# Three score banks in turned order, and the row of maxima in another of them, in an attention layer over 4,096 keys

## What is computed

```
energy = einsum('nqhd,nkhd->nhqk', q, k)            # 16 heads of 16 features
energy = where(mask == 0, -1e20, energy)            # one mask for both batches
attn   = softmax(energy / sqrt(256), axis=keys)     # over 4,096 keys
x      = x + (einsum('nhql,nlhd->nqhd', attn, v).reshape(...) @ w_out.T + b_out)
```

## Time and profile before

| | |
|---|---|
| median of 3 runs | 1079.19 us (1078.21 to 1080.05) |
| the profiled execution | 1083.97 us, its span 1082.3 us |
| PE busy | 964.2 us (89% of the span) |
| DVE busy | 595.2 us (55%) |
| ACT busy | 443.2 us (41%) |
| the units of layer 4 | from 458 us to 918 us of the span |
| time of one unit inside | 14.32 us (transposes of two units start at 701.51 and 715.83 us) |

### The profile page before, as it was taken

How to read it: one execution, slowest core, us unless ns; L and a number is a source line. 1 busy time by engine, 2 the same in 40 slices (tenths; PEclk the granted TensorE clock), 3 DMA queues, 4 the chain that set the end, 5 groups by cost and what they waited for, 6 DMA issues and landing times.

```text
span 1082.3 us, 19810 instructions
## 1 busy us (share of the span) xinstructions
PE 964.2 (89%) x7079; PEld 557.6 (52%) x7080; DVE 595.2 (55%) x1485; ACT 443.2 (41%) x812; POOL 97.5 (9%) x132
## 2 busy tenths in 40 slices
PE   6999989979899992599999999999999998755978
PEld 5888855545566662234444444444444443534547
DVE  3445434643122224677777777777777772294762
ACT  3443424521122210366666666666666665201011
POOL 1323210004011111000000000000000000100000
PEclk9999996989899997699999999999999999876998
DMA  7744865053003535825455444445555400800000
GB/s 273 241 160 172 321 264 223 2 187 98 11 30 115 157 128 113 180 37 74 74 74 72 68 65 65 62 65 72 72 72 72 68 6 20 187 0 1 0 1 20
DMA packets 76266, 106.09 MB, mean 98 GB/s; under 512 B 27478, under 2 KB 62647, under 8 KB 72186
## 3 DMA queue, kind: packets, MB, share of 16 engines
q1 hardware_dynamic: 70818, 89.38, 37.2%
q0 software_dynamic: 5200, 15.61, 3.7%
q10 hardware_dynamic: 200, 0.44, 0.1%
HBM read 83.40 MB, written 20.22 MB: 96 GB/s over the span
## 4 chain that ended last, share of the span: by engine, by line
PE 79%; DVE 5%; DMA 4%; issue 4%; ACT 4%; SPq 3%; ACTq 0%; POOL 0%; another core or an unknown queue 0%; POOLq 0%; DVEq 0%
PE bank L1191 12%; PE bank L1212 11%; PE bank L1200 8%; PE bank L1096 7%; PE bank L1169 5%; PE bank L1368 4%; PE bank L1120 4%; PE bank L903 3%; PE bank L890 3%; ACT region L805 2%; PE bank L985 2%; PE bank L1069 2%; PE bank L1223 2%; PE bank L994 1%; PE bank L1404 1%
## 5 line engine op out<-in xcount | busy, mean ns | idle before, releaser
L805 ACT ACTIVATE region<-bank 128x512 f32<-128x512 f32 x512 | 277.9, 595 | 173.4 <-PE bank L1200 173.4
L1690 DVE CUSTOM_DVE_ANT_0 xnT<-bank,region 128x1024 bf16<-128x1024 f32 x128 | 156.1, 1220 | 88.2 <-issue 88.2
L1191 PE MATMUL bank<-region 128*128 (+1 forms) x1024 | 163.4, 277 | 13.6 <-ACT region L805 12.6
L1690 DVE CUSTOM_DVE_ANT_0 region<-bank,region 128x1024 bf16<-128x1024 f32 x128 | 156.3, 1221 | 0.4
L1191 PEld LDWEIGHTS bank<-region 128*128 128x128 bf16 x1024 | 67.7, 97 | 139.8 <-ACT region L805 61.7
L1212 PE MATMUL bank<-region 128*32 128x256 f32 x2048 | 138.6, 385 | 0.0
L1200 PE MATMUL bank<-region,identb 64*64 64x512 bf16 x1024 | 105.4, 402 | 0.0
L1169 PE MATMUL bank<-region,xnT 64*128 64x512 bf16 x248 | 75.5, 385 | 5.0 <-DMA xnT<-region 5.0
L1212 PEld LDWEIGHTS bank<-region 128*32 128x32 f32 x2048 | 58.9, 109 | 34.2 <-ACT region L805 14.5
L1096 PE MATMUL bank<-region 128*128 x240 | 74.8, 465 | 1.2 <-DVE region L1612 1.2
L1171 PE MATMUL bank<-region,xnT 64*128 64x512 bf16 x248 | 75.5, 385 | 0.0
(11 more groups left out here) (317 smaller groups left out, 1151.1 us busy)
## 6 DMA issues: line engine op xcount, KB each, us to landing
region<-keys_split SPq DMA_DIRECT2D x224, 128.0 KB, 4.9
region<-in_ctx SPq DMA_DIRECT2D x32, 512.0 KB, 4.5
keys_split<-region POOLq DMA_DIRECT2D x48, 256.0 KB, 4.1
region<-in_L_ffn_we_gate SPq DMA_DIRECT2D x8, 688.0 KB, 8.7
region<-in_L_ffn_we_up SPq DMA_DIRECT2D x8, 688.0 KB, 9.8
region<-in_L_ffn_we_down SPq DMA_DIRECT2D x8, 640.0 KB, 9.3
region<-in_mask_1x1xSxS_ik SPq DMA_DIRECT2D x1, 4096.0 KB, 16.8
mask_kept<-region SPq DMA_DIRECT2D x1, 2048.0 KB
```

Of the source, the lines that this page charges most:

```text
L805: nc.scalar.activation(prob4[n % PROBS].rearrange("p a b -> p (a b)"), bank[:, SCORE4[n], :], ACT.Exp, scale=SCALE4).then_inc(exp4_ready, 1)
L1191: mm(bank[:, SCORE4[n], k * S:(k + 1) * S], slab[s][:, t * P:(t + 1) * P], qT4[:, bass.ds(u, 1), :].rearrange("p o q -> p (o q)"), start=( ...
L1690: v.tensor_tensor_reduce(out=junk[q], in0=bank[:, 3 + 2 * q:5 + 2 * q, :].rearrange("p a b -> p (a b)"), in1=maskN[:, q, 2 * c * CH:2 * (c ...
```

## The change

The order of the three banks is turned from half 8 on: the halves 8 to 15 take the banks 0, 2, 1, 0, 2, 1, 0, 2. The transposed maxima go into bank 1 (`NEG4`), and the wait ahead of them is for that bank's last half. `LAST_USE4` is worked out from the order by the same line as before, and so are all waits in `score_half`. No instruction is added or taken away.

```diff
-SCORE4 = (0, 1, 2, 0, 1, 2, 0, 1, 2, 0, 1, 2, 0, 1, 2, 1)
+SCORE4 = (0, 1, 2, 0, 1, 2, 0, 1, 0, 2, 1, 0, 2, 1, 0, 2)
+NEG4 = 1
 LAST_USE4 = [max(m for m in range(n - HALVES, n) if SCORE4[m % HALVES] == SCORE4[n]) for n in range(HALVES)]
@@ negmax_T
-                    pe.wait_ge(exp4_ready, HALVES * u + LAST_USE4[0] + 1)
+                    pe.wait_ge(exp4_ready, HALVES * u + LAST_USE4[NEG4] + 1)
                 for q in range(QT):
-                    last = nc.tensor.transpose(bf16_bank(SCORE4[0])[NEG_ROWS, q * P:(q + 1) * P], negparts[:, q, 0:2],
+                    last = nc.tensor.transpose(bf16_bank(SCORE4[NEG4])[NEG_ROWS, q * P:(q + 1) * P], negparts[:, q, 0:2],
                                                identb[:, :])
@@ negmax_row
-                              bf16_bank(SCORE4[0])[NEG_ROWS, 0:S]).then_inc(negT_ready, 1)
+                              bf16_bank(SCORE4[NEG4])[NEG_ROWS, 0:S]).then_inc(negT_ready, 1)
```

## The result

| | before | after |
|---|---|---|
| median (range) | 1077.12 us (1073.08 to 1080.05, 6 runs) | 1060.29 us (1057.07 to 1065.55, 6 runs) |
| profiled execution | 1083.97 us, span 1082.3 us | 1057.07 us, span 1055.4 us |
| one inner unit | 14.32 us | 13.83 us |

The ratio of after to before is 0.9855, with a 95% interval of 0.982 to 0.9891. It is the ratio of the mean times, 1061.17 to 1076.75 us, which lie 15.6 us apart; the medians lie 16.8 us apart. The forecast, 1063.4 to 1079.19, is a ratio of 0.9854.

A forecast was written before the change was run, and what follows sets the result against it. TensorE, busy 89% of the span, was taken as the bound, stalling before half 15. 30 units x 0.49 plus 2 x 0.54 gave 15.8 us, so 1079.19 - 15.8 = 1063.4 us, range 1061.8 to 1067.0 us.

The forecast's parts named there:

- The step of the sum: Group 7 of each inner unit: the stall before half 15 goes whole, 0.49 us a unit, 14.7 us over 30 units.
- The last two units: Units 30 and 31, without maxima between groups 6 and 7: 0.54 us saved each, together 1.1 us.
- rival B: Group 7: the idle column is right, a unit gives only 0.31 us, 1068.8 us in all; chance 0.04.
- the wait for 13 ahead of the transpose: Transpose after group 7 waits one exponential later than before; half 13 is seen 0.17 us early, cost 0.
- rival C: The stall moves to the transpose or half 0; if 0.49 us came back, 1079 us; chance 0.06.
- VectorE's copy (A): Copy of the maxima row holds group 0; unmoved, 0.29 us a unit returns, 1073.0 us; cover put at 0.20; chance 0.06.
- the maxima behind the copy: Second pair of maxima, needing banks freed by VectorE's `take_max`: thin cover of 0.1 us, nothing changes in it.
- The clock (D): TensorE loses its clock as it gets fuller, making the kernel slower; chance 0.04.
- the level: Whole-kernel time before the change, taken as the runs' median, 1079.19 us, 4.8 us below the profiled execution.
- The forecast's own scatter: Whole kernel: +-1 us from the runs, plus 0.02 us of rounding in each of 32 units, 0.6 us.

The follow-up runs named there:

- Plain turns: Banks 0, 1, 2 in plain turn through the unit without reversal, row of maxima in bank 1, against the kernel before: 1072.07 us, ratio 0.9932.
- the added instructions: Changed kernel plus a VectorE reduction ahead of the maxima's copy, against the kernel before: 128 x 256 floats 1068.63 us, 128 x 512 floats 1075.61 us.
- row_only: Row of maxima moved to bank 1, banks in the old order, against the kernel before: 1132.85 us, ratio 1.0503.
- turn_only: Turned bank order with the row of maxima left in bank 0, against the kernel before: 1087.37 us, ratio 1.009.
- turn_at_14: Bank order reversed from half 14 on instead of half 8, against the kernel before: 1067.61 us, ratio 0.9912.

## Why the prediction came out as it did

**The change's own size was right.** The step of the sum, 0.49 us in a unit from 0.54 against 1.03 us, was measured as 14.32 - 13.83 = 0.49 us. The last two units, put at 0.54 us each, gave 0.49 too. Over all units the traces give 15.7 us for a forecast of 15.8. Reversing at half 11 puts just this gap into group 5. That settles rival B: the idle column shows 0.31 us there too, and the unit loses 0.49. The prediction went by the start times; the idle column is too small here, and the earlier trace rows show why: the two matmuls of half 14 are drawn as 0.39 us where the next is due after 0.27, which hides 0.12 us, and from half 15 to the mask it is 0.32 us in place of 0.27. With 0.31 that makes 0.48 us.

**Why no wait took its place.** Plain turns show what half 0 pays when it waits for half 15 (0.38 us), turning at half 14 what group 7 pays for the first of a pair (0.22 us), the turn without the row's bank what the transpose pays for half 14 (0.75 us). With the wait for 13 ahead of the transpose there is no gap in the trace; its margin of 0.17 us held. So rival C fell: these waits can bite, and the changed order places each where it doesn't.

**VectorE's copy (A)** has less cover than I worked out, 0.09 us and not 0.20. It cost nothing, for the copy did move with the transpose. My term came from the first unit, which is written out, with 0.15 us between the end of the copy and the weights; in the loop it is 0.25. The thinnest cover is that of the maxima behind the copy, 0.03 us: the added instructions cost the unit their lateness less these 0.03 us, not less the cover of group 0. The forecast did not depend on it only because the copy kept its distance to the transpose.

**The clock (D)** stayed at 1.00 from 462 to 876 us, with TensorE busy for all but 0.36 us. Behind the first unit it fell only in the kernel with the longest gap (1.17 us idle), and in eleven of its units. So here a fuller TensorE, busy for 413.64 of 414 us, did not bring a clock below 1.00, and the 1.17 us of idle time went with one of 0.90 in these eleven units; that the idle time is the cause is argued from one kernel, and its other units behind the first had such gaps too (1.17 us in the loop, 1.26 us in the written-out ones) at a clock of 1.00. What brought the 0.60 of the earlier trace rows was not looked into.

**What failed is the level and its scatter.** The prediction said "The forecast's own scatter is that of the runs, +-1 us" and took 1079.19 us as the level, from three runs within 1.8 us. Its own table had a fourth execution, the profiled one, at 1083.97 us, so four executions spanned 5.8 us. The three further runs of before in the comparison took 1073.08, 1073.91 and 1076.03 us, all below the first three. In 56 runs of the kernel before, over this study, the median is 1078.0 us, the range 1069.7 to 1086.8 us, and the middle eight tenths reach from 1073.9 to 1083.4 us. All six gave 1077.12 us, 2.1 us lower than the level used; that with the forecast's 15.8 us gives 1061.3 us, already below the range, and still 1.0 us over the measured median. The other 1.0 us is the scatter of six runs of the changed kernel, which reach from 1057.07 to 1065.55 us: the interval of the ratio (0.982 to 0.9891) is 7.7 us wide, and by the twelve runs' median of 1062.4 us the same forecast would have held. That it missed by 1.5 us was bad luck, but a range of 1.6 us below the forecast left it to luck. The scatter's place is in the traces: in the two of before the units repeat to 0.1 us in 445, while over all traces the stretch ahead of them varies by 10.7 us, going with the granted clock and with a stop that four traces have and nine haven't. The prediction had both on its own page, as stretches with a clock below 1.00 and an "issue" share of 4% in the chain, and gave them no scatter. What sets off the stop, and what sets the clock there, is open.

## What to carry to other kernels

In a ring of buffers written in pairs, what a wait costs is not told by its distance in the ring but by the work that stands between: a distance of two cost 0, 0.03, 0.22 or 0.49 us by its place in the unit. List for each place when the releasing instruction ends against when the waiting one is due, put the short distances behind the longest work, and check the second user of a bank (here the row of maxima) by the same list. Where two waits followed each other here, those of group 0 and of the maxima, their lateness didn't add up: with group 0 late by 0.09 us and the maxima by 0.15 the unit was 0.15 us longer, set by the one with the least cover. Price a stall by start times of the same piece with and without it; and take the scatter of a level from the parts that are not tied to the change, not from three runs that agree.

## What the runs showed of the hardware

- The second exponential of a pair ended 0.05 us ahead of the matmuls that waited for it inside group 7 (before: 715.12 and 715.17 us) and at the transpose (row_only: 646.59 and 646.64). At the head of a unit with plain turns it was 0.26 us to the weights in three units of four in the loop (642.22 and 642.48), 0.15 us in the fourth (571.38 and 571.53), and in a written-out unit 0.12 us to the weights and 0.15 to the matmuls (883.23, 883.35 and 883.38).
- Behind the first exponential of a pair, with its end taken at half of the pair's time, it was 0.11 us to the weights (turn_only's transpose: 640.95 and 641.06; turn_at_14's group 7: 645.23 and 645.34).
- With 1.17 us of idle time before each transpose (1.26 us in the written-out units) TensorE was granted 0.90 of its clock over each of eleven of 31 units (row_only; 0.50 from 647 to 650 us in one of them) and 1.00 in others of the same kernel. With gaps of 0.31 us (before, 472 to 902 us) and of 0.69 us before each transpose (turn_only, 500 to 860 us) the clock was 1.00.
- Ahead of layer 4, where nothing was changed, the thirteen traced executions differed by 10.7 us in the start of the first transpose (446.3 to 457.0 us), with a granted clock of 0.92 to 0.94 over these 446 us.
